# Causal mask of a fused attention block: a minimum on VectorE in place of mask products on TensorE, with the tile sums and the ends of the stages reordered

## The chip, the cores and the metric

The kernel runs on one core of one Trainium2 chip. The metric is device time in microseconds (us) of one execution; lower is better. TensorE is called PE below (PEld is its weight loads), VectorE DVE, ScalarE ACT, GpSimd POOL, and SyncE, which issues the DMAs here, SP.

## What is computed

Two rows of 2048 tokens of width 256 go through a pre-norm attention layer of 16 heads of width 64, and then through a linear layer:

```python
qkv = layernorm(x) @ W_qkv                       # [2, 2048, 3 * 1024]
score = einsum('bihd,bjhd->bijh', q, k) / 8
mask = tril(ones((l, l)))                        # keys after the query are left out
wmat = softmax(score * mask + 1e30 * (mask - 1), axis=2)
x = x + einsum('bijh,bjhd->bihd', wmat, v).reshape(b, l, 1024) @ W_out
W2 = W + up_aux @ (lora_up @ (lora_down @ down_aux))
x = x + layernorm(x) @ W2.T + b
```

## The kernel before

The kernel is written with an explicit order for each engine and explicit semaphores; nothing is scheduled by a tool. It has three stages, each one a block in which all engines run their own lists; between two blocks all engines wait for each other.

**First stage** (`project_qkv`): layernorm, then q, k and v for 8 tiles of 512 tokens. ACT and DVE copy each product out of PSUM into three stage buffers each, SP stores them (line 249). At the end of SP's list, lines 258 to 260 wait until every store has landed. Near the end the stage already loads q and k of the first item and finds its row maxima.

**Second stage** (`attention`): 16 items, one for each pair of heads and batch row. An item has 40 units (t, j): for each tile t of 512 queries (t from 0 to 3) the blocks j of 128 keys, j from 0 to 4t + 3. Units are numbered s, tile t starting at s = 0, 4, 12, 24. The last four units of a tile lie on the diagonal; they are called d0 to d3 here, and need 512, 384, 256 and 128 query columns for each of the two heads. For a unit

- PE makes the scores (`score_unit`, L791: four terms for each head, the last adds minus the row maximum), and on the diagonal adds four small products (L798, the constants `late_keys` and `pick`) that put -3e38 where the key comes after the query;
- ACT takes the exponential into one of 8 buffers `probs` (L921);
- PE multiplies by v into `o_acc` (`pv_unit`, L855);
- the sum of the exponentials is built: by POOL for the units before the diagonal (L1093, into `sum_pool`), by DVE on the diagonal (L1012 in tile 0, L1018 for d0, which reads `sum_pool`, and L1023 for d1 to d3, into `sum_dve`).

PE works in pairs of units: scores of the units s + 2 and s + 3, then the v products of s and s + 1. In between stand the row-maximum products of the next item (`chunk`, L819 and, on their diagonal, L827) into a ring of three PSUM banks, placed by the fixed table of `plan_chunks` (written "B" for a whole chunk and "s" for a narrow one); DVE reduces each (L990), and frees its bank thereby. In the last item nothing follows, so there are none.

Once a tile is summed, PE adds over the partitions (`denominators`, L865), ACT copies the row (L950), SP spreads it over the partitions through DRAM, DVE takes the reciprocal (L1043), SP brings it back (L713), POOL normalises (`normalise`, L1077, ten units into the next tile), and SP stores the tile of o (L699). POOL also makes the low halves of q and k for the next item at eight fixed units (L676, units 3, 8 to 11 and 20 to 22). The last item also splits W_out and loads and splits the first tile of o for the third stage (L722, L943, L1037).

POOL starts the sum of a tile (unit j = 1) once DVE has read `sum_pool` in d0 of the tile before.

**Third stage** (`project_and_ffn`): for 8 tiles of 512 tokens the output projection (`out_project`, L1271), layernorm and the linear layer (L1294). ACT and DVE split each tile of o into a high and a low half first (L1335, L1371). The last tile of o of the stage before is finished at its start (`finish_last_o`, L1223 to L1236), and only behind it SP loads the tiles 2 and 3 of o (L1191).

DVE's list for a unit, before:

```python
for here in places[1:] if s % 2 else places[:1]:
    for k in here:
        reduce_chunk(...)
if j >= NB * t:
    add_unit(n, s)
for late in late_tile(n, s - 5, previous):
    reciprocals(*late)
```

## Time and profile before

| | us |
|---|---|
| median of 3 runs (1955.82 to 1957.56) | 1955.83 |
| the profiled execution, its own time | 1958.16 |
| its span, first to last instruction | 1955.9 |
| PE busy | 1839.4 (94%) |
| DVE busy | 1247.7 (64%) |
| POOL busy | 1073.3 (55%) |
| ACT busy | 806.6 (41%) |

The first stage takes the time up to about 313 us, the second from there to about 1790, the third the rest. "Busy" of PE is modelled and counts overlapping instructions once. The mean granted PE clock is 0.987 of full speed.

### The profile page before, as it was taken

Reading aid. Unit: us, or ns where it says so; the run is one execution under the profiler, and the core shown is the slowest. Engines: PE = TensorE matmul, PEld = TensorE weight load, DVE = VectorE, ACT = ScalarE, POOL = GpSimd, SP = SyncE. Lnnn points to the kernel's source line nnn. Section 1 sums busy time; section 2 is a strip of 40 time slices with the busy share of each in tenths; the row PEclk is TensorE's granted clock in tenths of the full one; section 3 lists DMA queues with packets and bytes.
Section 4 is the critical chain, followed back from the end, with each engine's and each line's share of the span. In section 5 each row is a group of like instructions: output and inputs, shape, how many; then the busy total and the mean of one; then the engine's idle time right before and its main releaser. Section 6 shows DMA issues by size and latency. Waiting matters only on the chain. (4 is left out here: it accounts for less than half of the span.)

```text
span 1955.9 us, 34245 instructions
## 1 busy us (share of the span) xinstructions
PE 1839.4 (94%) x13464; PEld 1130.9 (58%) x13464; DVE 1247.7 (64%) x2024; ACT 806.6 (41%) x982; POOL 1073.3 (55%) x583
## 2 busy tenths in 40 slices
PE   7999998999999999999999999999999999997798
PEld 5877775555555555555555555555555555545697
DVE  5465643767676767667676767676767677632465
ACT  3222123444545454544545454545454545453121
POOL 1001002767586857667676767686867667575111
PEclk9999998999999999999999999999999999998899
DMA  5646445212121221212121212121221211031451
GB/s 204 227 175 227 162 167 173 66 45 66 50 66 56 59 66 45 66 45 78 54 73 37 77 39 72 45 69 47 66 72 45 66 45 50 18 117 47 172 194 54
DMA packets 150782, 171.33 MB, mean 88 GB/s; under 512 B 44618, under 2 KB 91744, under 8 KB 150624
## 3 DMA queue, kind: packets, MB, share of 16 engines
q1 hardware_dynamic: 150624, 169.15, 27.4%
q8 instruction: 108, 1.77, 0.4%
q14 instruction: 50, 0.41, 0.1%
HBM read 97.02 MB, written 71.57 MB: 86 GB/s over the span
## 5 line engine op out<-in xcount | busy, mean ns | idle before, releaser
L990 DVE TENSOR_REDUCE f_part_max<-b_ring 128x1 f32<-128x512 f32 (+3 forms) x1200 | 675.2, 604 | 323.6 <-PE b_ring L819 224.3
L921 ACT ACTIVATE b_probs<-b_scores 128x1024 f32<-128x1024 f32 (+3 forms) x640 | 567.5, 899 | 611.9 <-PE b_scores L791 357.6
L1093 POOL TENSOR_TENSOR b_sum_pool<-b_sum_pool,b_probs 128x1024 f32<-128x1024 f32 x288 | 687.0, 2385 | 61.6 <-ACT b_probs L921 31.3
L791 PE MATMUL b_scores<-f_split 64*128 64x512 f32 (+2 forms) x1920 | 269.6, 383 | 9.1 <-ACT b_probs L921 5.5
L791 PE MATMUL b_scores<-b_split 64*128 64x512 f32 (+2 forms) x1920 | 269.2, 382 | 2.8 <-ACT b_probs L921 2.6
L855 PE MATMUL b_o_acc<-b_probs,f_v_in 128*64 128x512 f32 (+3 forms) x1280 | 270.5, 544 | 0.0
L855 PE MATMUL b_o_acc<-b_probs,b_v_in 128*64 128x512 f32 (+3 forms) x1280 | 269.0, 541 | 0.0
L1093 POOL TENSOR_TENSOR b_sum_pool<-b_probs 128x1024 f32<-128x1024 f32 x48 | 116.0, 2417 | 264.0 <-ACT b_probs L921 264.0
L1023 DVE TENSOR_TENSOR g_sum_dve<-g_sum_dve,b_probs 128x768 f32<-128x768 f32 (+2 forms) x192 | 231.3, 1205 | 30.2 <-ACT b_probs L921 24.4
L791 PEld LDWEIGHTS b_scores<-b_split 64*128 64x128 f32 x1920 | 166.3, 186 | 50.5 <-issue 21.2
L791 PEld LDWEIGHTS b_scores<-f_split 64*128 64x128 f32 x1920 | 168.0, 187 | 45.8 <-issue 21.1
L819 PE MATMUL b_ring<-b_split 64*128 64x512 f32 (+2 forms) x640 | 142.8, 433 | 28.3 <-DVE f_part_max L990 27.6
L348 DVE COPY a_stage_d<-a_made 128x512 f32<-128x512 f32 x96 | 66.2, 691 | 142.1 <-PE a_made L293 142.0
L819 PEld LDWEIGHTS b_ring<-b_split 64*128 64x128 f32 x640 | 64.8, 183 | 146.7 <-issue 143.3
L819 PE MATMUL b_ring<-f_split 64*128 64x512 f32 (+2 forms) x560 | 125.5, 434 | 25.6 <-DVE f_part_max L990 24.8
L348 ACT COPY a_stage_a<-a_made 128x512 f32<-128x512 f32 x96 | 56.5, 589 | 225.6 <-PE a_made L293 225.6
L855 PEld LDWEIGHTS b_o_acc<-b_probs,b_v_in 128*64 128x64 f32 x1280 | 77.8, 136 | 111.2 <-issue 86.7
L855 PEld LDWEIGHTS b_o_acc<-b_probs,f_v_in 128*64 128x64 f32 x1280 | 77.9, 136 | 110.1 <-issue 86.8
L819 PEld LDWEIGHTS b_ring<-f_split 64*128 64x128 f32 x560 | 57.0, 184 | 128.8 <-issue 126.1
L791 PE MATMUL b_scores<-f_shift,p_first_row 64*128 64x512 f32 (+2 forms) x640 | 120.3, 364 | 0.0
L791 PE MATMUL b_scores<-b_shift,p_first_row 64*128 64x512 f32 (+2 forms) x640 | 120.2, 363 | 0.0
L676 POOL TENSOR_TENSOR b_split<-f_raw,b_split 128x512 fp32r<-128x512 f32 x64 | 81.5, 1297 | 54.8 <-ACT b_split L903 54.8
(135 smaller groups left out, 2250.4 us busy)
## 6 DMA issues: line engine op xcount, KB each, us to landing
f_raw<-k_t SPq DMA_DIRECT2D x32, 512.0 KB, 4.8
f_raw<-q_t SPq DMA_DIRECT2D x32, 512.0 KB, 5.6
g_recip<-r_t SPq DMA_DIRECT2D x128, 128.0 KB, 3.0
o_t<-g_o_norm SPq DMA_DIRECT2D x64, 256.0 KB, 2.0
q_t<-a_stage_a SPq DMA_DIRECT2D x32, 256.0 KB, 2.3
q_t<-a_stage_d SPq DMA_DIRECT2D x32, 256.0 KB, 2.1
k_t<-a_stage_a SPq DMA_DIRECT2D x32, 256.0 KB, 2.0
k_t<-a_stage_d SPq DMA_DIRECT2D x32, 256.0 KB, 2.0
```

The source lines that it names most:

```text
L348: copy(stage[e][s][:], made[:, g % BANKS, :]).then_inc(emptied[e], 1)
L676: vec.tensor_tensor(lo[u][:, cols], raw[p][:, which, inner], halves(hi[u][:, cols]), ALU.subtract).then_inc(split_lo, 1)
L791: last = nc.tensor.matmul(scores[s % 2][:, h, lo:TILE], lhs, b[u][head(h), queries], start=(term == 0), stop=(term == 3 and not diagonal))
L819: last = nc.tensor.matmul(rowwise[h][:, 0:wide], q_hi[u][head(h), ib * P:(ib + 1) * P], k_hi[u][head(h), c * TILE:c * TILE + wide], start= ...
L855: last = nc.tensor.matmul(o_acc[head(h), off:], v_in[u][:, j, head(h)], probs[s % PR][:, h, off:], start=(j == 0), stop=(j == NB * t + NB ...
L921: nc.scalar.activation(probs[s % PR][:, :, off:], scores[s % 2][:, :, off:], ACT.Exp, scale=scale).then_inc(exp_done, 1)
L990: nc.vector.tensor_reduce(part_max[:, h, ib, c:c + 1], rowwise[h][:, 0:width], AX.X, ALU.max).then_inc(chunk_reduced, 1)
L1023: nc.vector.tensor_tensor(sum_dve[t % 2][:, :, off:], sum_dve[t % 2][:, :, off:], probs[s % PR][:, :, off:], ALU.add).then_inc(dve_added, 1)
L1093: nc.gpsimd.tensor_tensor(sum_pool[:], first, probs[s % PR][:], ALU.add).then_inc(pool_added, 1)
```

## The change

The mask products L798 of the scores go. Instead DVE takes, for each diagonal unit, the minimum of the square of 128 by 128 exponentials (both heads) and a constant `allowed`, which is 3e38 where the key is allowed and 0 where it isn't. PE's v product of a diagonal unit and DVE's own add wait for that (`cleared`). DVE does the minimum as the first thing of its unit, ahead of the chunk reductions.

```diff
-                    diagonal = j >= NB * t
...
-                    if diagonal:
-                        for side in range(2):
-                            cols = slice(off + side * D, off + (side + 1) * D)
-                            for h in range(2):
-
-                                last = nc.tensor.matmul(scores[s % 2][:, h, cols], late_keys(h, side),
-                                                        consts["pick"][head(h), :], start=False, stop=(side == 1))
...
-                    pe.wait_ge(exp_done, n * U + s + 1 + 2)
+                    if j >= NB * t:
+                        pe.wait_ge(cleared, clear_before[n, s] + 1)
+                    else:
+                        pe.wait_ge(exp_done, n * U + s + 1 + 2)
...
+                def clear_later_keys(n, s):
...
+                    dve.wait_ge(exp_done, n * U + s + 1 + 2)
+                    nc.vector.tensor_tensor(probs[s % PR][:, :, off:off + P], probs[s % PR][:, :, off:off + P], allowed[:],
+                                            ALU.min).then_inc(cleared, 1)
...
+                        if j >= NB * t:
+                            clear_later_keys(n, s)
```

POOL's first add of a tile waits until DVE has finished the whole sum of the tile before, not only its d0:

```diff
-                                pool.wait_ge(dve_added, n * DIAG + NB * (t - 1) + 1 + NB)
+                                pool.wait_ge(dve_added, sum_ready[n, t - 1])
```

In the last tile of the last item DVE adds also the last four units ahead of the diagonal (j = 8 to 11), starting its own sum there, and adds POOL's sum once, behind d1. In the last item POOL normalises four units earlier:

```diff
+    LATE_FULL = 4
+    def dve_adds(n, s):
+        t, j = units[s]
+        return j >= NB * t or (n == LAST_ITEM and t == TI - 1 and j >= NB * t - LATE_FULL)
...
-                        for late in late_tile(n, s - 10, previous):
+                        for late in late_tile(n, s - (10 if following else 6), previous):
                             normalise(*late)
```

The waits for the first stage's stores move from the end of its SP list to the start of the second stage's, ahead of the loads of q and k of the second item. In the third stage SP issues the loads of o for the tiles 2 and 3 ahead of `finish_last_o`, and the load of x for tile 2 behind it:

```diff
                 load_x(0, 0)
+
+                wait_apart(sp, o_lo_ready, PARTS, first_loaded[0], 16)
...
-                finish_last_o()
-
-                wait_apart(sp, o_lo_ready, PARTS, first_loaded[0], 16)
                 load_o(2, 0, slice(0, KC), o_loaded[0])
-                step(0, 0, True, True, False)
+                step(0, 0, True, False, False)
+                finish_last_o()
+                wait_apart(sp, x1_ready, 1 + 2, first_loaded[0], 16)
+                load_x(2, 0)
```

How the lists stand. DVE in tile 1 of an item, from d0 on, before (L990 reduces chunks, L1018 and L1023 are the adds of d0 to d3, L1043 the reciprocal):

```order
L1018 TENSOR_TENSOR g_sum_dve<-b_sum_pool,b_probs 128x1024
L990 TENSOR_REDUCE f_part_max<-b_ring 128x1 x2
L1023 TENSOR_TENSOR g_sum_dve<-g_sum_dve,b_probs 128x2x384
L1043 RECIPROCAL g_recip_spread<-g_den_spread 128x8
L990 TENSOR_REDUCE f_part_max<-b_ring 128x1 x2
L1023 TENSOR_TENSOR g_sum_dve<-g_sum_dve,b_probs 128x2x256
L990 TENSOR_REDUCE f_part_max<-b_ring 128x1 x2
L1023 TENSOR_TENSOR g_sum_dve<-g_sum_dve,b_probs 128x2x128
```

The same place in the changed kernel (L1037 is the minimum, L1017 reduces, L1055 and L1060 are the adds, L1086 the reciprocal):

```order
L1037 TENSOR_TENSOR b_probs<-b_probs,b_allowed 128x2x128
L1017 TENSOR_REDUCE f_part_max<-b_ring 128x1 x2
L1055 TENSOR_TENSOR g_sum_dve<-b_sum_pool,b_probs 128x1024
L1037 TENSOR_TENSOR b_probs<-b_probs,b_allowed 128x2x128
L1017 TENSOR_REDUCE f_part_max<-b_ring 128x1 x2
L1060 TENSOR_TENSOR g_sum_dve<-g_sum_dve,b_probs 128x2x384
L1086 RECIPROCAL g_recip_spread<-g_den_spread 128x8
L1037 TENSOR_TENSOR b_probs<-b_probs,b_allowed 128x2x128
L1017 TENSOR_REDUCE f_part_max<-b_ring 128x1 x2
L1060 TENSOR_TENSOR g_sum_dve<-g_sum_dve,b_probs 128x2x256
L1037 TENSOR_TENSOR b_probs<-b_probs,b_allowed 128x2x128
```

Four minimums stand in the list now; that of d1 stands right behind the add of d0.

POOL's list of the last item, tiles 1 to 3, before (L1093 adds, L1077 normalises the tile before):

```order
L1093 TENSOR_TENSOR b_sum_pool<-b_sum_pool,b_probs 128x1024 x2
L1077 TENSOR_TENSOR g_o_norm<-g_o_raw,g_recip 128x512
L1093 TENSOR_TENSOR b_sum_pool<-b_probs 128x1024
L1093 TENSOR_TENSOR b_sum_pool<-b_sum_pool,b_probs 128x1024
L1077 TENSOR_TENSOR g_o_norm<-g_o_raw,g_recip 128x512
L1093 TENSOR_TENSOR b_sum_pool<-b_sum_pool,b_probs 128x1024 x5
L1077 TENSOR_TENSOR g_o_norm<-g_o_raw,g_recip 128x512
L1093 TENSOR_TENSOR b_sum_pool<-b_probs 128x1024
L1093 TENSOR_TENSOR b_sum_pool<-b_sum_pool,b_probs 128x1024 x9
L1077 TENSOR_TENSOR g_o_norm<-g_o_raw,g_recip 128x512
L1093 TENSOR_TENSOR b_sum_pool<-b_sum_pool,b_probs 128x1024
```

The same in the changed kernel (L1138 adds, L1123 normalises):

```order
L1138 TENSOR_TENSOR b_sum_pool<-b_sum_pool,b_probs 128x1024
L1123 TENSOR_TENSOR g_o_norm<-g_o_raw,g_recip 128x512
L1138 TENSOR_TENSOR b_sum_pool<-b_sum_pool,b_probs 128x1024
L1123 TENSOR_TENSOR g_o_norm<-g_o_raw,g_recip 128x512
L1138 TENSOR_TENSOR b_sum_pool<-b_probs 128x1024
L1138 TENSOR_TENSOR b_sum_pool<-b_sum_pool,b_probs 128x1024 x5
L1123 TENSOR_TENSOR g_o_norm<-g_o_raw,g_recip 128x512
L1138 TENSOR_TENSOR b_sum_pool<-b_sum_pool,b_probs 128x1024
L1138 TENSOR_TENSOR b_sum_pool<-b_probs 128x1024
L1138 TENSOR_TENSOR b_sum_pool<-b_sum_pool,b_probs 128x1024 x5
L1123 TENSOR_TENSOR g_o_norm<-g_o_raw,g_recip 128x512
L1138 TENSOR_TENSOR b_sum_pool<-b_sum_pool,b_probs 128x1024
```

The last tile has 7 adds in place of 11, and each normalisation now stands ahead of adds that it stood behind.

## Rows read from the trace of the kernel before

**Rows 1.** The page, part 1: busy us (share of the span) xinstructions.
```profile
PE 1839.4 (94%) x13464; PEld 1130.9 (58%) x13464; DVE 1247.7 (64%) x2024; ACT 806.6 (41%) x982; POOL 1073.3 (55%) x583
```
**Rows 2.** Line 1012, one copy for each item: duration, first and last start.
```profile
L1012 DVE COPY g_sum_dve<-b_probs x16: 694/694/695, 319.3 to 1704.6; 128x1024 f32<-128x1024 f32 x16
```
**Rows 3.** Waits of the whole span: us in total, times, longest us.
```profile
PE b_ring L819 <- DVE f_part_max L990: 52.4, 71, 1.0
```
**Rows 4.** Timeline of PE, item 5, tile 1: start us, us, instruction [idle before].
```profile
804.47 0.23 PE L798 MATMUL b_scores<-p_pick,p_late_keys 64*128 64x64 bf16 x4
804.54 0.60 PE L791 MATMUL b_scores<-b_split 64*128 64x256 f32 x6
...
805.54 1.73 PE L855 MATMUL b_o_acc<-b_probs,b_v_in 128*64 128x512 f32 x8
...
814.05 0.50 PE L819 MATMUL b_ring<-f_split 64*128 64x512 f32 x2 [0.81 <-DVE f_part_max L990]
```
**Rows 5.** Timeline of DVE, the same stretch.
```profile
811.36 2.34 DVE L1023 TENSOR_TENSOR g_sum_dve<-g_sum_dve,b_probs 128x256 f32<-128x256 f32 x1
```
**Rows 6.** Timeline of POOL, the same stretch.
```profile
803.36 1.28 POOL L1077 TENSOR_TENSOR g_o_norm<-g_o_raw,g_recip 128x512 f32<-128x512 f32 x1
804.60 1.28 POOL L676 TENSOR_TENSOR f_split<-f_raw,f_split 128x512 fp32r<-128x512 f32 x1
811.02 2.39 POOL L1093 TENSOR_TENSOR b_sum_pool<-b_probs 128x1024 f32<-128x1024 f32 x1 [5.14 <-ACT b_probs L921]
```
**Rows 7.** Line 1023: duration ns min/median/max over its three widths.
```profile
L1023 DVE TENSOR_TENSOR g_sum_dve<-g_sum_dve,b_probs x192: 424/943/2569, 323.9 to 1790.0; 128x768 f32<-128x768 f32 x64, 128x512 f32<-128x512 f32 x64, 128x256 f32<-128x256 f32 x64
```
**Rows 8.** Groups by line and shape: busy us, mean ns of one, idle before.
```profile
L1023 DVE TENSOR_TENSOR g_sum_dve<-g_sum_dve,b_probs 128x256 f32<-128x256 f32 x64 | 116.3, 1817 | 2.0
```
**Rows 9.** Timeline of the last item, tile 2: PE, DVE, POOL.
```profile
1748.85 1.72 PE L855 MATMUL b_o_acc<-b_probs,b_v_in 128*64 128x512 f32 x8
...
1749.89 1.23 DVE L1018 TENSOR_TENSOR g_sum_dve<-b_sum_pool,b_probs 128x1024 f32<-128x1024 f32 x1 [5.62 <-POOL b_sum_pool L1093]
1751.22 3.19 DVE L1023 TENSOR_TENSOR g_sum_dve<-g_sum_dve,b_probs 128x768 f32<-128x768 f32 x3
...
1750.63 1.63 POOL L1077 TENSOR_TENSOR g_o_norm<-g_o_raw,g_recip 128x512 f32<-128x512 f32 x1 [0.85 <-DMA g_recip<-r_t]
```
**Rows 10.** The last item, tile 1: timeline of PE, then windows (PEclk third from last).
```profile
1733.18 1.08 PE L865 MATMUL b_ring<-g_sum_dve,p_ones 128*64 128x512 f32 x4 [2.42 <-DVE g_sum_dve L1023]
...
1734.00:1736.00 2.00, 2.00 (x12) 1.49 (x12) 0.00 (x0) 0.62 (x2) 0.00 (x0) 0.65 0.45 126
1736.00:1738.00 2.00, 2.00 (x10) 1.01 (x10) 0.00 (x0) 1.32 (x2) 1.90 (x2) 0.50 0.00 0
```
**Rows 11.** Timeline of the end of the second stage: PE's last products, DVE, the third stage.
```profile
1779.43 2.37 PE L855 MATMUL b_o_acc<-b_probs,b_v_in 128*64 128x512 f32 x16
...
1786.81 1.22 DVE L1018 TENSOR_TENSOR g_sum_dve<-b_sum_pool,b_probs 128x1024 f32<-128x1024 f32 x1 [13.67 <-POOL b_sum_pool L1093]
...
1790.89 0.55 PE L1271 MATMUL c_y<-f_shift,f_split 128*128 128x256 f32 x1 [9.08 <-DVEq L1407]
```
**Rows 12.** Window of the third stage: length, busy of PE, PEld, DVE, ACT, POOL; PEclk; DMA.
```profile
1791.00:1796.00 5.00, 5.00 (x24) 5.00 (x25) 1.52 (x1) 3.44 (x1) 0.00 (x0) 0.50 0.72 210
```
**Rows 13.** Timeline of the third stage: SP, ACT, DVE and PE.
```profile
1823.25 0.37 SPq L1191 DMA_DIRECT2D f_raw<-o_t  x1
...
1817.39 1.02 ACT L1345 COPY c_xt<-c_turned 128x1024 f32<-128x1024 f32 x1 [3.96 <-PE c_turned L1282]
1832.38 3.60 ACT L1335 CAST f_split<-f_raw 128x4096 fp32r<-128x4096 f32 x1 [13.97 <-DMA f_raw<-o_t]
...
1836.02 4.42 DVE L1371 TENSOR_TENSOR f_split<-f_raw,f_split 128x4096 fp32r<-128x4096 f32 x1 [20.04 <-ACT f_split L1335]
...
1840.49 0.80 PE L1271 MATMUL c_y<-f_shift,f_split 128*128 128x256 f32 x2 [14.23 <-DVE f_split L1371]
```
**Rows 14.** Timeline of ACT at the start of the second stage.
```profile
322.07 1.04 ACT L903 CAST b_split<-f_raw 128x1024 fp32r<-128x1024 f32 x1 [2.84 <-DMA f_raw<-q_t]
```

102 lines of the change are left out of this document (69 added, 33 removed).

## The prediction

> **What bounds the kernel now.** I read the page first, then PE's waits over the whole span, then the timeline of one item around its tile ends, then the two block borders. The page shows PE busy for 1839.4 us, 94% of the span, with the next engine, DVE, at 64% [rows 1]: whatever takes work or idle time from PE counts in full, and nothing else does. The second stage is regular: the copy that opens each item starts at 319.3 in the first and 1704.6 in the last, so an item takes (1704.6 - 319.3)/15 = 92.35 us [rows 2]. One wait of PE inside the items matters: for a bank of the ring that DVE has yet to reduce, 52.4 us in 71 places, none over 1.0 us [rows 3]; over 15 items with a ring that is 3.5 us each.
>
> Where that comes from is seen at the end of tile 1 of item 5. POOL starts the next tile's sum at 811.02 and needs 2.39 us [rows 6]. DVE's add of d3 starts at 811.36, right behind it, and takes 2.34 us [rows 5], though the shortest add of line 1023 takes 0.424 us [rows 7]. POOL's add ends at 813.41; 813.41 - 811.36 = 2.05, and about 0.3 more is DVE's own work. So DVE stood until POOL was done, and the chunk reduction behind it kept PE waiting 0.81 us [rows 4]. It is the rule, not an exception: the 64 adds of this shape have a mean of 1817 ns [rows 8]. In these rows an add of DVE and an operation of POOL never run side by side; the one that is there first holds the other up for its whole length.
>
> **The mask products.** They go from PE. Four of them stand between 804.47 and 804.54 [rows 4]: 0.07 us a unit, since they run behind the larger ones. 16 units an item give 1.1 us, 16 items 18 us, all on PE's path.
>
> **POOL held behind DVE's sum.** The add of d3 then finds no POOL add, and takes about 0.45 us for 1.82 [rows 7, 8]. The ring waits should go nearly all: -3.5 us an item [rows 3]. POOL's first add starts about 1 us later, and so do the splits and the normalisation behind it; POOL's slack (1073.3 us busy of 1955.9 [rows 1]) covers that inside the tile, but these later operations now lie where the diagonal is.
>
> **The minimum.** The trace has no minimum. It has the shape of the smallest add of line 1023 (128x256, two operands in SBUF), so it is bounded by 0.42 us below (that add undisturbed) and 2.57 us above (the longest add of that line, which stood behind POOL) [rows 7]; I take 0.42 of its own, and work out its waits one by one. DVE has room for 16 x 0.42 = 6.7 us an item. For PE what counts is when the minimum is done, since the v product of a diagonal unit waits for it now. That of d0 and of d2 have a pair's scores as cover. That of d1 stands right behind the add of d0 on DVE, and the v product of d1 is due 0.9 us after that of d0. So the add of d0 (1.23 us undisturbed [rows 9]) enters PE's path, and with it whatever holds the add.
>
> Replay of tile 1 of item 5, all by durations of the rows. POOL's chain there ended with a split, a normalisation at 803.36 and a split at 804.60, 1.28 us each [rows 6]; by the later first add it stands some 0.6 us later, while PE, without picks and ring waits, comes 1.4 us earlier, the products of 805.54 [rows 4] at 804.15. The add of d0 is ready at 804.1, and finds the normalisation on (to 805.2): it ends at 806.3. POOL's last split, waiting since 805.2, then goes first, ahead of the minimum of d1: 807.55, minimum 807.85. PE wants it at 805.06: a wait of 2.9 us with the semaphore. In tile 2 the same replay gives 2.15, and 0.2 for d3. In tiles 0 and 3 the exponential and POOL's last add are both over by some 2 to 3 us when the products are due: nothing. Sum +5.25 us an item. If DVE kept the port from the add of d0 to the minimum, each wait would be about 0.65 us: these are the ends of this term, +1.3 and +5.25, and from the upper end on a lost clock (below). I take 5.25, since in the last item's tile 2 POOL's normalisation, waiting since 1750.63, did go between DVE's adds: three adds took 3.19 us, where the widest takes 0.94 undisturbed and the narrowest 0.42 [rows 7, 9], so about 1.1 of it was POOL's.
>
> By the Trainium skill, "SBUF — State Buffer", section "Who interferes with whom", the port pair is an exclusive lock that goes to whoever issues first, for the whole instruction. By that rule, the trace agrees for the adds. Taken to the letter, POOL's split, waiting since 805.2, goes ahead of the minimum, which gives the 5.25; were the lock given to DVE each time, the sum would be the fast rival's below.
>
> An item: -1.1 - 3.5 + 5.25 = +0.6; 15 items: **+9 us**.
>
> **The last item and the end of the stage.** Before, PE waited 2.42 us there for the sum of a tile, and the granted clock then showed 0.65 and 0.50 of full speed for 4 us [rows 10], which is 2 x 0.35 + 2 x 0.5 = 1.7 us lost: my price of such a fall. POOL's earlier normalisation takes this wait away, and the minimums bring two waits of 1.8 and 1.0 in the same tile by the same replay: -2.4 - 1.7 + 2.8 = -1.3. In tile 2 the add of d0 waited 5.62 us for POOL's sum, to 1749.89, and nothing of PE hung on it; the v product of d1 came at about 1748.85 + 0.9 = 1749.8 [rows 9]. Now the normalisation stands ahead of POOL's last add and the minimum of d1 behind the add of d0: 1749.89 + 1.3 + 1.23 + 0.4 = 1752.8, 3 us late. PE arrives some 2 us earlier too (1.3 as above, and 0.7 of picks by then), while POOL, which adds without a break there, does not: +5, and a fall, +1.7. Picks -1.1. Last item: +4.3; its ends are -1.1 - 4.1 = -5.2, if POOL is out of the way in both tiles, and +6.
>
> At its end PE is done with the products at 1781.8, but DVE starts on POOL's late sum at 1786.81, and PE starts the third stage at 1790.89, 9.08 us idle [rows 11]. In the changed kernel POOL has four adds of 2.4 us fewer, and DVE adds its sum once, behind d1, so what is left behind the last product is one small add and the border itself, about 1.95 us: -7.1. The slow clock of 0.50 in the 5 us after the gap [rows 12] is then not due: -2.6. Last item and border together: **-5.4**.
>
> **The third stage.** SP issues the load of the second tile of o at 1823.25, behind the finishing of the last tile; ACT waits 13.97 us for it (1832.38), DVE splits from 1836.02, and PE stands from 1826.3 to 1840.49, 14.23 us [rows 13]. Moved ahead, the load is issued at about 1794.3 and has landed long before ACT is free behind its copy of 1817.39: high half 1818.4 to 1822.0 (3.60), low half to 1826.5 (4.42), PE on at 1826.6. So -13.9, and the slow start behind the gap goes (as at the block border: -1.6), +0.3 for ACT and DVE being in the way of a smaller step: **-15.2**. Moved back on SP's list are the finishing of the last tile and the load of x of tile 2, both needed only many us later. The load shares the DMA engines with the weights issued at the start; it took 9.1 us before, from 1823.25 to ACT's start, and has 24 us now.
>
> **Between the first and second stage.** The stores' waits now stand ahead of the second item's loads. ACT still waits 2.84 us for the first loads of this stage until 322.07 [rows 14], and those loads wait on the same stores. I take **-0.3**; the ends are 0 and -2.84. The constant `allowed` is made by POOL at the start, covered by the same wait.
>
> **The sum.** The profiled execution took 1958.16, 2.3 above the median 1955.83. 1958.16 - 0.3 + 9 - 5.4 - 15.2 = 1946.3, which is 11.9 less; against the median, 1955.83 - 11.9 = **1944**.
>
> **The rivals.**
> *Slower: the clock falls at the new wait.* The wait of 2.9 us in tile 1 is longer than the one of 2.42 that was followed by a slow clock [rows 10]. If each costs a fall, 1.7 x 15 = 25 us more: 1969. If in tile 2 POOL's normalisation goes first too (+1.3) and the clock falls there (+1.7), 4.7 x 15 = 70 more: 2014. It decides from 0.8 us an item beyond my sum, since 11.9/15 = 0.79. For it: the idle time is longer and recurs. Against: the sum of d0 sits in a stretch where PE was fully busy before, and the last item, without the ring's products, may be special. Chance 0.27.
> *Faster: DVE keeps the port.* The waits are 1.3 us an item: 3.95 less, -59 at most; PE then runs earlier against ACT and some of it returns. With a quarter returned, about 45 less than my sum: 1899; halfway, where only one of the two tiles loses the race, 1922. For it: POOL needs a cycle through its own semaphore between operations, DVE doesn't. Against: the 3.19 us of [rows 9]. Chance 0.25.
> *No change: the ends give nothing.* The third stage's gap could stay, if the early load waits for its buffer or for the weights on the DMA engines; then 15.2 is missing: 1959, or 1955 where a fourth of it comes. For it: only that the load is a big one. Against: the 24 us. Chance 0.08.
> The forecast, 1937 to 1951, has 0.40.
>
> **How the numbers follow.** The range takes the fast rival in at its lower end, 1899, rounded to 1900, and the first half of the slow one, 1969, to 1975; what is left out is the doubled clock fall and a fast case without any return. A measurement of this kernel can tell about 0.2%, 3.9 us. Faster by over that (below 1951.9): 0.40 - 0.05 for a forecast missed towards the border, + 0.25 = 0.60; the slow rival ends above 1959.7 nearly always, and with the slow end of the no-change case: 0.27 + 0.04 = 0.31; same: 0.04 + 0.05 = 0.09.
>
> **What would show it.** Right: L798 gone; the add of 128x256 near 0.45 us; L819's wait for DVE nearly gone; new waits of PE's v products for the minimum (L1037), 2 to 3 us each in tiles 1 and 2, none in 0 and 3; items of about 93 us between the copies; PE's gap near 1826 gone, and the one at the border down to about 2 us. Each of these at another size mis-sizes its own term. Slow rival: granted clock below full speed behind the waits. Fast rival: minimums of d1 that start right behind the add of d0, items near 89.5. Wrong altogether: items unchanged with the waits gone, which would mean that another engine than PE paces them.

## The result, and the profile after

The changed kernel takes 1999.98 us (median of 4 runs, 1997.09 to 2007.53), the kernel before 1956.69 in the same measurement: a ratio of 1.0226, 95% interval 1.0196 to 1.0256. It is slower by 2.3%. The forecast was 1944, range 1900 to 1975. The profiled execution took 1997.09 us with a span of 1995.1, 39.2 more than the 1955.9 before.

Part 1 of the page, to be held against [rows 1]:

```profile
PE 1856.7 (93%) x12440; PEld 1116.3 (56%) x12440; DVE 1355.8 (68%) x2285; ACT 802.7 (40%) x982; POOL 1102.1 (55%) x582
```

PE has 1024 instructions fewer (256 units of 4 mask products) and is "busy" 17 us longer. That can't be more work: work went away, and the granted clock was lower (0.97 for 1.00 of full speed between 340 and 1680 us). The waits of PE over the whole span, beside [rows 3] (engine, tile, line, releaser: us in total, times, longest):

```profile
PE b_o_acc L886 <- DVE b_probs L1037: 83.4, 40, 6.3
PE b_scores L826 <- ACT b_probs L948: 15.0, 16, 6.1
...
PE b_ring L847 <- DVE f_part_max L1017: 8.6, 26, 1.7
```

The ring waits went from 52.4 us to 8.6 as forecast, and 83.4 us of waiting for the minimum came. Item 5, tile 1 again, beside [rows 4 to 6]; PE, then DVE, then POOL:

```profile
816.92 1.08 PE L886 MATMUL b_o_acc<-b_probs,b_v_in 128*64 128x512 f32 x4
...
820.69 1.34 PE L886 MATMUL b_o_acc<-b_probs,b_v_in 128*64 128x384 f32 x4 [2.69 <-DVE b_probs L1037]
```
```profile
816.91 2.33 DVE L1055 TENSOR_TENSOR g_sum_dve<-b_sum_pool,b_probs 128x1024 f32<-128x1024 f32 x1
819.16 1.48 DVE L1037 TENSOR_TENSOR b_probs<-b_probs,b_allowed 128x256 f32<-128x256 f32 x1
```
```profile
816.89 1.26 POOL L1123 TENSOR_TENSOR g_o_norm<-g_o_raw,g_recip 128x512 f32<-128x512 f32 x1
818.12 2.24 POOL L709 TENSOR_TENSOR f_split<-f_raw,f_split 128x512 fp32r<-128x512 f32 x1
...
827.53 2.38 POOL L1138 TENSOR_TENSOR b_sum_pool<-b_probs 128x1024 f32<-128x1024 f32 x1 [7.18 <-DVE g_sum_dve L1060]
```

This is the replay of the prediction, instruction by instruction. The add of d0 and POOL's normalisation start together (816.91 and 816.89); POOL works 1.26 us and the add is done after 2.33. POOL's split then goes ahead of the minimum of d1, which takes 1.48 us for 0.42 of its own. PE waits 2.69 us, where the prediction had 2.9. The last row shows the hold: POOL's first add starts at 827.53, behind DVE's whole sum, and the 128x256 add, 1817 ns in the mean before [rows 8], is cheap:

```profile
L1060 DVE TENSOR_TENSOR g_sum_dve<-g_sum_dve,b_probs 128x256 f32<-128x256 f32 x64 | 26.7, 417 | 0.6
```

What came on top is in the clock. Windows of 2 us around this wait, and around the end of that of tile 2 (852.5); the third number from the right is the granted clock:

```profile
819.00:821.00 2.00, 0.31 (x2) 0.20 (x4) 2.00 (x4) 0.00 (x0) 1.35 (x1) 0.99 0.40 133
821.00:823.00 2.00, 2.00 (x12) 0.84 (x10) 1.75 (x5) 0.00 (x0) 0.00 (x0) 0.50 0.00 0
823.00:825.00 2.00, 2.00 (x14) 1.58 (x14) 1.77 (x4) 0.39 (x1) 0.00 (x0) 0.66 0.07 2
852.00:854.00 2.00, 1.51 (x6) 0.32 (x6) 2.00 (x5) 0.00 (x0) 0.16 (x1) 0.50 0.52 160
...
856.00:858.00 2.00, 2.00 (x12) 1.57 (x10) 0.42 (x2) 1.02 (x1) 0.00 (x0) 0.50 0.63 205
```

The clock falls from 2.4 to 1.2 GHz at the wait and stays there for 3.4 us. In the 15 items with a ring there are 30 waits for the minimum of d1, of 1.57 to 2.69 us; at 21 of them such a slow stretch begins, between 0.9 us before the wait's end and 1.7 us behind it, and a 22nd came behind a ring wait of 1.69 us; five of the 22 are twice as long as the others, 6.8 us for 3.4.

Slow time multiplied by what is missing of full speed gives 46.1 us in the items, 27 times 1.7. The clock cost less than that, as is seen between items of one run that have like waits: 1.2 us in experiment 6, 1.5 in experiment 3, and 1.35 here for a further 3.4 us (items 6 and 12, with 6.8 us of slow clock, took 96.2 and 96.3; items 3, 5, 8 and 11, with 10.2, took 97.6). By these prices the clock cost 32 to 41 us.

To compare kernels I cut every trace at the same places: the first v product of item 0, that of item 15, PE's last v product, PE's first product of the third stage. The first two start at 325.2 and 1706.4 before (92.09 an item, where the prediction had 92.35 by DVE's copies); after:

```profile
323.59 1.97 PE L886 MATMUL b_o_acc<-b_probs,f_v_in 128*64 128x512 f32 x3
...
1756.51 1.72 PE L886 MATMUL b_o_acc<-b_probs,b_v_in 128*64 128x512 f32 x8
```

| us | before | after | difference |
|---|---|---|---|
| to item 0 | 325.2 | 323.6 | -1.6 |
| one item (15 of them) | 92.09 | 95.53 | +3.44, in all +51.6 |
| of it, by the clock | 0 | 2.2 to 2.7 | +32 to 41 in all |
| last item | 75.4 | 86.8 | +11.4 |
| border gap of PE | 9.1 | 1.1 | -8.0 |
| third stage | 165.1 | 150.7 | -14.4 |
| span | 1955.9 | 1995.1 | +39.2 |

The two block borders and the third stage gave 24 us; the items took 51.6, of which 32 to 41 is the clock, and the last item 11.4.

### The profile page after: what moved, and what is told of

It is laid out like the page before. It is cut to its first block and busy times, and to the rows that moved or that the text cites. A ratio compares the mean times of both kernels' runs of the same rounds, so it can differ in the third digit from the quotient of the medians.

```text
span 1995.1 us, 32457 instructions
## 1 busy us (share of the span) xinstructions
PE 1856.7 (93%) x12440; PEld 1116.3 (56%) x12440; DVE 1355.8 (68%) x2285; ACT 802.7 (40%) x982; POOL 1102.1 (55%) x582
## 5 line engine op out<-in xcount | busy, mean ns | idle before, releaser
L1017 DVE TENSOR_REDUCE f_part_max<-b_ring 128x1 f32<-128x512 f32 (+3 forms) x1200 | 675.9, 605 | 340.7 <-PE b_ring L847 245.6
L1138 POOL TENSOR_TENSOR b_sum_pool<-b_sum_pool,b_probs 128x1024 f32<-128x1024 f32 x284 | 678.0, 2387 | 37.0 <-POOL b_sum_pool L1138 1.4
L886 PE MATMUL b_o_acc<-b_probs,b_v_in 128*64 128x512 f32 (+3 forms) x1280 | 281.5, 555 | 45.0 <-DVE b_probs L1037 44.8
L886 PE MATMUL b_o_acc<-b_probs,f_v_in 128*64 128x512 f32 (+3 forms) x1280 | 279.2, 552 | 38.7 <-DVE b_probs L1037 38.6
L1138 POOL TENSOR_TENSOR b_sum_pool<-b_probs 128x1024 f32<-128x1024 f32 x48 | 115.1, 2398 | 324.7 <-DVE g_sum_dve L1060 303.2
L826 PE MATMUL b_scores<-f_split 64*128 64x512 f32 (+2 forms) x1920 | 274.0, 391 | 12.6 <-ACT b_probs L948 10.8
L826 PE MATMUL b_scores<-b_split 64*128 64x512 f32 (+2 forms) x1920 | 273.2, 390 | 4.3 <-ACT b_probs L948 4.2
L1037 DVE TENSOR_TENSOR b_probs<-b_probs,b_allowed 128x256 f32<-128x256 f32 x256 | 194.2, 759 | 27.2 <-ACT b_probs L948 26.2
L826 PEld LDWEIGHTS b_scores<-f_split 64*128 64x128 f32 x1920 | 173.6, 194 | 54.8 <-ACT b_probs L948 19.4
L826 PEld LDWEIGHTS b_scores<-b_split 64*128 64x128 f32 x1920 | 172.0, 192 | 57.6 <-issue 20.3
L1060 DVE TENSOR_TENSOR g_sum_dve<-g_sum_dve,b_probs 128x768 f32<-128x768 f32 (+3 forms) x196 | 145.6, 743 | 3.2
```

Of the source, the lines that this page charges most:

```text
L826: last = nc.tensor.matmul(scores[s % 2][:, h, lo:TILE], lhs, b[u][head(h), queries], start=(term == 0), stop=(term == 3))
L886: last = nc.tensor.matmul(o_acc[head(h), off:], v_in[u][:, j, head(h)], probs[s % PR][:, h, off:], start=(j == 0), stop=(j == NB * t + NB ...
L1017: nc.vector.tensor_reduce(part_max[:, h, ib, c:c + 1], rowwise[h][:, 0:width], AX.X, ALU.max).then_inc(chunk_reduced, 1)
L1037: nc.vector.tensor_tensor(probs[s % PR][:, :, off:off + P], probs[s % PR][:, :, off:off + P], allowed[:], ALU.min).then_inc(cleared, 1)
L1060: nc.vector.tensor_tensor(sum_dve[t % 2][:, :, off:], sum_dve[t % 2][:, :, off:], probs[s % PR][:, :, off:], ALU.add).then_inc(dve_added, 1)
L1138: nc.gpsimd.tensor_tensor(sum_pool[:], first, probs[s % PR][:], ALU.add).then_inc(pool_added, 1)
```

## The experiments

All ratios are against runs of the kernel before on the same chip; the cuts are those of the table above. "Clock" is the slow time in the 15 items multiplied by what was missing of full speed, in us: 1.7 for a stretch of 3.4 us, more than it cost.

| kernel | median | ratio (95%) | item | waits for min / ring, tiles 1 and 2, an item | clock |
|---|---|---|---|---|---|
| changed | 1999.98 | 1.0226 (1.0196-1.0256) | 95.53 | 4.67 / 0.4 | 46.1 |
| minimums of a pair first | 1944.7 | 0.9948 (0.9932-0.9965) | 92.28 | 0 / 4.6 | 1.7 |
| POOL not held | 1967.57 | 1.0068 (1.0050-1.0086) | 93.40 | 2.50 / 0 | 0 |
| before, POOL held | 1927.65 | 0.9863 (0.9847-0.9880) | 89.92 | - / 1.46 | 8.5 |
| before, block ends | 1942.51 | 0.9933 (0.9917-0.9950) | 92.11 | - / 0.7 | 0 |
| reductions, then adds | 1960.61 | 1.0022 (1.0012-1.0032) | 93.29 | 0 / 4.9 | 10.2 |
| first in tile 1 alone | 1963.55 | 1.0043 (1.0029-1.0058) | 93.12 | 2.06 / 2.4 | 15.4 |
| POOL behind the minimum | 2088.32 | 1.0673 (1.0655-1.0691) | 101.66 | 2.7 / 7.2 | 81.9 |
| normalisation back | 1994.68 | 1.0221 (1.0181-1.0260) | 95.39 | 4.63 / 0.3 | 46.1 |
| minimum between | 1959.65 | 1.0019 (0.9995-1.0043) | 93.70 | 0.7 / 3.4 | 32.4 |
| products kept | 1905.9 | 0.9749 (0.9733-0.9766) | 89.95 | - / 1.36 | 10.2 |
| products kept, early norm. | 1911.91 | 0.9761 (0.9733-0.9788) | 90.19 | - / 1.50 | 11.9 |
| POOL light | 1885.38 | 0.9636 (0.9620-0.9652) | 88.23 | 1.02 / 0 | 0 |
| products kept, POOL light | 1870.0 | 0.9554 (0.9538-0.9570) | 87.67 | - / 0 | 0 |

(The ring waits at tile starts, 2.8 us an item, are there where POOL isn't held.)

**1. The minimum ahead of the add.**

```diff
-                        if j >= NB * t:
+                        if j >= NB * t and s % 2 == 0:
                             clear_later_keys(n, s)
+                            clear_later_keys(n, s + 1)
```

> The changed kernel with one thing moved: on DVE both minimums of a pair of diagonal units come first, so that of d1 stands ahead of the add of d0 and not behind it. Theory A (PE waits for the minimum of d1 because it stands behind an add that has to wait for POOL, and each such wait is followed by a slow clock): PE's wait for the minimums falls from 83.4 us to under 10, the slow-clock stretches inside the items go, an item takes about 92.1 - 1.1 (picks) - 2.8 (ring waits) = 88.2 us for 95.5, and the time is about 1998 - 15 x 7.3 - 8 in the last item = 1880 us. Theory B (256 minimums and a later POOL load the shared port, wherever they stand): the total of DVE's and POOL's work is the same, so items stay above 94 and the time above 1970.

Measured: 1944.7. The wait for the minimum is gone in the items, and so is the slow clock (1.7 us of it left), which is theory A. But the item takes 92.28 and not 88.2, so neither theory's number was hit: PE waits for the ring instead.

```profile
PE b_ring L847 <- DVE f_part_max L1017: 71.2, 93, 1.5
...
PE b_o_acc L886 <- DVE b_probs L1037: 10.3, 4, 5.3
```

Its DVE shows why: the two minimums take 2.88 us together, and the reductions stand behind them.

```profile
801.08 2.88 DVE L1037 TENSOR_TENSOR b_probs<-b_probs,b_allowed 128x256 f32<-128x256 f32 x2
803.88 1.27 DVE L1017 TENSOR_REDUCE f_part_max<-b_ring 128x1 f32<-128x512 f32 x2
805.08 2.31 DVE L1055 TENSOR_TENSOR g_sum_dve<-b_sum_pool,b_probs 128x1024 f32<-128x1024 f32 x1
```

So A holds for the clock and for where the wait was, and B has a share: as long as something holds DVE there, order only chooses who waits.

**2. Without the hold.**

```diff
-                                pool.wait_ge(dve_added, sum_ready[n, t - 1])
+                                pool.wait_ge(dve_added, sum_pool_read[n, t - 1] if t > 1 else dve_before[n, 0] + 1)
```

> The changed kernel, but POOL's first add of a tile waits only for DVE's read of its sum, as in the kernel before. Theory A: POOL's splits and normalisation stand about 1 us earlier, but still beside the add of d0, and PE meets the ring waits again; the waits for the minimum fall to 1.5 to 2.5 us each in tiles 1 and 2, and are still followed by a slow clock: items of 94 to 96 us, 1985 to 2005 in all. Theory C (holding POOL is what pushed its work into the diagonal, and alone makes the loss): the waits for the minimum fall below 0.7 us, no slow clock, items of about 92, 1945.

Measured: 1967.57, between the two theories, with the waits and the clock as neither had them. The waits for the minimum of d1 are 1.11 and 1.39 us in the mean, and none of them was followed by a slow stretch. Windows of this run, from just before the wait in item 5's tile 1 and tile 2 on:

```profile
812.00:816.00 4.00, 2.98 (x26) 1.98 (x28) 4.00 (x9) 0.61 (x1) 0.69 (x1) 1.00 0.08 4
842.00:846.00 4.00, 3.28 (x28) 2.04 (x28) 3.86 (x10) 0.98 (x2) 0.00 (x0) 1.00 0.94 199
```

The hold makes each wait about 1.1 us longer (2.35 and 2.32), and with the longer waits the slow clock comes. That the lengthening is due to PE coming sooner and POOL's splits later was argued and not tested apart.

**3. The hold alone**, in the kernel before.

```diff
-                                pool.wait_ge(dve_added, n * DIAG + NB * (t - 1) + 1 + NB)
+                                pool.wait_ge(dve_added, n * DIAG + NB * t + NB)
```

> The kernel before, with POOL held behind the whole of DVE's sum and nothing else. Theory A: PE's ring waits fall from 52.4 us to under 12 (8.6 in the changed kernel), nothing of PE waits for the sum of a diagonal, items take 92.1 - 2.8 = 89.3 us and the time is about 1956 - 42 = 1914 us. Theory C: the later POOL work costs PE elsewhere (exponentials wait for their buffer, sums come late): items stay above 91.5 and the time above 1945.

Measured: 1927.65, 1.4% faster. The items go from 92.09 to 89.92. The ring waits at the tile starts are gone; one of 1.46 us in the mean stays at d2 of tile 1; after five of them, each of 1.94 to 1.96 us, the clock is slow (after the longest, 2.43, it is not). Items 4, 6, 8 and 12 with such a fall took 91.4 to 91.5, item 10 with the same wait and none took 89.9: a fall cost 1.5 us. The 1914 expected was missed by 14 us: the item came out 0.6 longer (9 us in all, the falls among it), and the border gap of PE grew from 9.08 to 11.97. The last cell of a 2 by 2 is now full (item, us): before 92.09, hold 89.92, minimum 93.40, both 95.53. Added up, hold and minimum would give 91.23; together they cost 4.3 us more, of which some 2 are the clock.

**4. The block ends alone**, in the kernel before: the waits for the stores moved, the loads of o ahead of `finish_last_o`.

```diff
                 load_x(0, 0)
+                wait_apart(sp, o_lo_ready, PARTS, first_loaded[0], 16)
...
-                finish_last_o()
-                wait_apart(sp, o_lo_ready, PARTS, first_loaded[0], 16)
                 load_o(2, 0, slice(0, KC), o_loaded[0])
-                step(0, 0, True, True, False)
+                step(0, 0, True, False, False)
+                finish_last_o()
+                wait_apart(sp, x1_ready, 1 + 2, first_loaded[0], 16)
+                load_x(2, 0)
```

> The kernel before, with only the waits for the stores moved and the third stage's loads reordered. Expected from the changed kernel's trace: first stage's border -1.8 us, third stage -14.3, nothing else: 1956 - 16 = 1940 us, PE's 14.2 us gap gone. Rival: the first border's gain came from the rest of the change (none of it here), then 1942; or the load of o takes its time from the border's other loads, then above 1945.

Measured: 1942.51, 0.7% faster; to item 0 it is 1.1 us less, the third stage 13.6. The gap of [rows 13] is gone from PE's waits, the border gap stays (8.8), since its part of the change isn't in this kernel.

**5. Adds behind both reductions.** DVE's order for a pair: two minimums, the reductions of both units, the two adds; in the last item four minimums before the adds, and the normalisation at its old place.

```diff
+                        if j >= NB * t and s % 2 == 0:
+                            clear_later_keys(n, s)
+                            clear_later_keys(n, s + 1)
                         for here in places[1:] if s % 2 else places[:1]:
...
                         if dve_adds(n, s):
-                            add_unit(n, s)
+                            waiting.append(s)
+                        if s % 2 and (following or j != NB * t + 1):
+                            for unit in waiting:
+                                add_unit(n, unit)
+                            waiting = []
```

> The changed kernel with DVE's order for each pair of diagonal units: both minimums, then the chunk reductions of both units, then both adds (in the last item all four minimums ahead of the four adds), and POOL's normalisation of the last item at its old place. Theory A (what costs is everything that PE waits for standing behind the add of d0, which meets POOL; with the minimums alone ahead, the ring's reductions paid it instead, 4.6 us an item in the run before): minimums and ring waits both under 0.7 us an item, no slow clock in the items; an item 92.1 - 1.1 - 2.8 = about 88.3 us, last item about 74 us for 86.8; in all 1998 - 15 x 7.2 - 12 = about 1878. Theory B (the shared port is loaded in any order): the reductions come in time but the adds run late and hold ACT's buffers or the denominators; items above 91, time above 1925.

Measured: 1960.61; theory A fails here by its number, and theory B's numbers hold (items above 91, time above 1925), but not its account, which had the reductions in time. The ring waits stay, 4.9 us an item. In tile 1 of item 5 the minimums themselves took 1.00 and 1.50 us for 0.42, each behind a split of POOL. Putting the adds last doesn't help when the first of DVE's two-operand instructions is already held.

**6. The minimum first in tile 1 alone.**

```diff
-                        if j >= NB * t:
+                        if j >= NB * t and t != 1:
                             clear_later_keys(n, s)
+                        if j >= NB * t and t == 1 and s % 2 == 0:
+                            clear_later_keys(n, s)
+                            clear_later_keys(n, s + 1)
```

> The changed kernel with the minimums of a pair ahead of the adds in tile 1 alone; tiles 2 and 3 as changed. Theory A (each wait of about 2 to 2.7 us is followed by its own slow stretch): PE's wait for the minimum of d1 in tile 1 goes (2.35 us an item), ring waits of some 2.4 us an item come in its place, in pieces; tile 2 keeps its 2.3 us. Slow stretches of 1.7 us fall from 27 to about 13 or 14: items 95.5 - 0.9 x 1.7 = about 94.0 us, 1975 in all. Rival (the clock falls because of both waits together): slow stretches under 4 in all, items about 92.5, 1952.

Measured: 1963.55, items of 93.12. Nine slow stretches, 15.4 us, between A's 13 and the rival's 4. Removing one of two waits an item removed more than half of them. The waits of the items 3 to 13 are nearly alike here: those with a fall took 93.45 to 93.77 us, those with none 92.41 to 92.49, so a fall cost 1.2 us in the mean.

**7. POOL's splits and normalisation behind the minimum of d1.**

```diff
+                        if t in (1, 2) and j == NB * t:
+                            pool.wait_ge(cleared, clear_before[n, s + 1] + 1)
                         if following and s in LO_SLOTS:
```

> The changed kernel, with POOL's splits and normalisation of tiles 1 and 2 held until the minimum of d1 is done, so that nothing of POOL can stand ahead of the add of d0 or of that minimum. Theory A (1.7 to 2.2 us of the wait are POOL's operation ahead of the add, and the one between add and minimum): the wait for the minimum falls from 2.35 and 2.32 us to about 0.6 each, and no slow clock follows; POOL's operations now meet the adds of d1 to d3 and cost ring waits of 1 us or so; items about 95.5 - 3.1 (clock) - 3.4 + 1 = 90 us, 1915 in all. Rival (the wait is DVE's own queue, the reductions and the add ahead of the minimum): the wait stays at 1.5 us or more in both tiles, items above 92.

The wait in question did what A says: 0.50 us in tile 1 and in tile 2, for 2.35 and 2.32. Yet the time is 2088.32. DVE of this run, tile 1:

```profile
850.59 1.22 DVE L1055 TENSOR_TENSOR g_sum_dve<-b_sum_pool,b_probs 128x1024 f32<-128x1024 f32 x1
851.72 0.42 DVE L1037 TENSOR_TENSOR b_probs<-b_probs,b_allowed 128x256 f32<-128x256 f32 x1
...
861.02 0.20 DVE L1086 RECIPROCAL g_recip_spread<-g_den_spread 128x8 f32<-128x8 f32 x1 [6.71 <-DMA g_den_spread<-g_den_row]
```
```profile
862.12 0.79 PE L847 MATMUL b_ring<-f_split 64*128 64x512 f32 x2 [6.68 <-DVE f_part_max L1017]
```

Add and minimum are free of POOL (1.22 and 0.42). But POOL's three splits start at 852.22, behind the minimum, and the normalisation only at 856.64. SP issues its store at 857.97 and behind it the small load of the denominators, for which the reciprocal on DVE waits 6.71 us, with the reductions behind it. I had costed this at ring waits of 1 us: the chain through SP was missed.

**8. The normalisation of the last item back at its place.**

```diff
-                        for late in late_tile(n, s - (10 if following else 6), previous):
+                        for late in late_tile(n, s - 10, previous):
```

> The changed kernel with POOL's normalisation of the last item at its old place, ten units into the next tile. As the prediction has it, the early normalisation of tile 1 stands ahead of POOL's last add of tile 2 there, and the minimum of d1 waits for it: the wait of 6.3 us falls by the 1.3 us of one normalisation to about 5, and the 2.4 us wait for the sum of tile 0 comes back: the last item stays within 2 us of 86.8. Rival (the early normalisation makes the 6.3 us wait): it falls below 3 us and the last item takes under 82 us.

The rival is right on the wait: that in tile 2 falls from 6.30 to 1.74 us. The last item falls only to 83.8, since the two waits in tile 1 grew from 3.1 to 3.9 us together and those of tile 3 from 2.9 to 3.7, so neither number of the last item was hit; the wait for the sum of tile 0 did not come back.

Where the 4.6 us come from is seen in the two traces. In both, one normalisation stands among POOL's adds of tile 2. In the changed kernel another one stands ahead of the first add, and waits for the load of its own reciprocals. The changed kernel, POOL, then DVE:

```profile
1783.88 1.27 POOL L1123 TENSOR_TENSOR g_o_norm<-g_o_raw,g_recip 128x512 f32<-128x512 f32 x1 [10.65 <-DMA g_recip<-r_t]
1785.11 2.40 POOL L1138 TENSOR_TENSOR b_sum_pool<-b_probs 128x1024 f32<-128x1024 f32 x1
...
1801.29 2.33 POOL L1138 TENSOR_TENSOR b_sum_pool<-b_sum_pool,b_probs 128x1024 f32<-128x1024 f32 x1
```
```profile
1779.97 0.42 DVE L1060 TENSOR_TENSOR g_sum_dve<-g_sum_dve,b_probs 128x256 f32<-128x256 f32 x1
...
1803.72 1.23 DVE L1055 TENSOR_TENSOR g_sum_dve<-b_sum_pool,b_probs 128x1024 f32<-128x1024 f32 x1 [5.82 <-POOL b_sum_pool L1138]
```

And POOL with the normalisation back:

```profile
1780.82 2.38 POOL L1138 TENSOR_TENSOR b_sum_pool<-b_probs 128x1024 f32<-128x1024 f32 x1 [9.38 <-DVE g_sum_dve L1060]
```

DVE's sum of tile 1 is done at 1780.4 in the changed kernel, and POOL's first add of tile 2 starts 4.7 us later: 3.5 of standing at the normalisation and 1.3 of doing it. With the normalisation back the add starts 0.1 us behind DVE's sum. POOL goes on almost without a break from there, and the wait of PE for the minimum of d1 is longer by as much, 6.30 us for 1.74.

**9. The minimum between.** On DVE: minimum of d0, its reductions, minimum of d1, add of d0; normalisation back.

```diff
-                        if j >= NB * t:
+                        if j >= NB * t and s % 2 == 0:
                             clear_later_keys(n, s)
...
+                        if j >= NB * t and s % 2 == 0:
+                            clear_later_keys(n, s + 1)
                         if dve_adds(n, s):
                             add_unit(n, s)
```

> The changed kernel with the minimum of d1 (and of d3) between the reductions of the even unit and the add of d0, so that it neither stands behind the add nor ahead of the reductions, and POOL's normalisation of the last item at its old place. Theory A: the wait for the minimum goes as with both minimums first (2.35 and 2.32 us an item to near nothing), and of the ring waits that came in its place there (4.6 us an item) the 1.4 and 0.7 us ahead of d0's product go too, since the reductions now come first; items 92.3 - 2.1 = about 90.2 us, 1912 in all. Theory B (the port is loaded in any order, the wait only moves): ring waits or waits for the minimum stay above 4 us an item and the items above 92, 1940 or more.

Measured: 1959.65, items of 93.70; B in its numbers (3.4 + 0.7 us of waits). The waits ahead of the product of d0 did go (1.41 to 0, 0.73 to 0.09), but those at d2 grew to 1.70 and 1.58 us, with 19 slow stretches. DVE, then POOL, of this run:

```profile
805.23 1.46 DVE L1037 TENSOR_TENSOR b_probs<-b_probs,b_allowed 128x256 f32<-128x256 f32 x1
806.61 1.27 DVE L1017 TENSOR_REDUCE f_part_max<-b_ring 128x1 f32<-128x512 f32 x2
807.81 1.52 DVE L1037 TENSOR_TENSOR b_probs<-b_probs,b_allowed 128x256 f32<-128x256 f32 x1
809.26 2.29 DVE L1055 TENSOR_TENSOR g_sum_dve<-b_sum_pool,b_probs 128x1024 f32<-128x1024 f32 x1
```
```profile
803.91 3.92 POOL L709 TENSOR_TENSOR f_split<-f_raw,f_split 128x512 fp32r<-128x512 f32 x3
807.79 1.27 POOL L1125 TENSOR_TENSOR g_o_norm<-g_o_raw,g_recip 128x512 f32<-128x512 f32 x1
809.01 1.45 POOL L709 TENSOR_TENSOR f_split<-f_raw,f_split 128x512 fp32r<-128x512 f32 x1
```

DVE's three instructions with two operands in SBUF each waited for one of POOL's: 1.46, 1.52 and 2.29 us where they need 0.42, 0.42 and 1.22, 3.2 us lost in all. Whichever stands last is late.

**10, 11. The mask products kept**, all else of the change; with the last item's normalisation at its old place, and at the new one.

```diff
+                    if diagonal:
+                        for side in range(2):
...
+                                last = nc.tensor.matmul(scores[s % 2][:, h, cols], late_keys(h, side),
...
-                    if j >= NB * t:
-                        pe.wait_ge(cleared, clear_before[n, s] + 1)
-                    else:
-                        pe.wait_ge(exp_done, n * U + s + 1 + 2)
+                    pe.wait_ge(exp_done, n * U + s + 1 + 2)
...
-                        if j >= NB * t:
-                            clear_later_keys(n, s)
```

> The changed kernel with the mask products on PE put back in place of the minimum; POOL still held, the last tile's adds shared with DVE, the block ends reordered; POOL's normalisation of the last item at its old place. From the runs so far: start of the items at 323.6, items of 89.9 us (as with POOL held alone), a last item of 73 to 74, a border gap of 1.1 and a third stage of 151: 323.6 + 1348.8 + 73.5 + 1.1 + 151 = 1898 for the span, a time of 1900 to 1903 us, the best so far. If the items get slower than 91, the rest of the change costs there too.

> The same, with the normalisation of the last item four units earlier as in the changed kernel. PE's product of d1 no longer hangs on DVE here, so the early normalisation can cost only through the sums: the wait of 1.0 us for the sum of tile 0 goes, nothing else comes; within 2 us of the run without it.

Measured: 1905.9 and 1911.91. The first is the best full kernel of this study, 2.5% faster than before, though 3 us over what I expected: the border gap is 6.4 us, not 1.1. PE is done with its products at 1746.5 there, and DVE's last adds end only at 1752.3:

```profile
1751.12 1.22 DVE L1062 TENSOR_TENSOR g_sum_dve<-g_sum_dve,b_probs 128x512 f32<-128x512 f32 x2
...
1752.81 0.77 PE L1313 MATMUL c_y<-f_shift,f_split 128*128 128x256 f32 x2 [6.35 <-DVEq L1449]
```

In the changed kernel DVE's last add ends at 1843.1, 0.3 us ahead of PE's last product, PE having waited 2.9 us for DVE's minimums in tile 3 by then. So the gap of 1.1 us is not the reordering's doing alone.

The medians of the two runs lie 6 us apart where I expected 2 at most. Their times overlap (1902.6 to 1914.04 against 1905.36 to 1910.01), so the time alone doesn't show that the early normalisation costs anything without the minimum. In the profile the last item was 3.2 us longer, and a wait of PE for the sum of tile 2 had grown from 0.4 to 3.1 us; POOL's first add of tile 2 stands behind a normalisation that waits for its load here too (10.30 us idle before it).

**12, 13. POOL's splits and normalisations made small**, in the changed kernel and in that of 10. Each works on 32 of its 512 columns; the rest of that work is left out, so these two kernels don't compute the layer, and their times serve as measurements only.

```diff
+            if vec is nc.gpsimd:
+                cols = slice(part * TILE, part * TILE + D // 2)
+                inner = slice(half * TILE, half * TILE + D // 2)
...
-                    nc.gpsimd.tensor_tensor(o_norm[:], o_raw[t % 2][:], recip[:], ALU.mult).then_inc(o_ready, 1)
+                    nc.gpsimd.tensor_tensor(o_norm[:, 0:D // 2], o_raw[t % 2][:, 0:D // 2], recip[:, 0:D // 2], ALU.mult).then_inc(o_ready, 1)
```

(The untouched columns are set to zero once, at the start of the stage.)

> The changed kernel, where each split of the next item's low halves and each normalisation on POOL works on 32 columns of its 512 (the rest of that work is left out, so the low halves and o are not those of the reference); every wait and the number of operations stay. Theory A (PE's waits come from POOL's full operations going on the shared port between DVE's): the wait for the minimum of d1 falls from 2.35 and 2.32 us to about 0.5 in each tile (DVE's add alone, as in the run with POOL's work held), the ring waits stay under 0.5, no slow clock in the items: items of 92.1 - 1.1 - 2.8 + 1.0 = about 89.2 us, 1998 - 15 x 6.3 = about 1903 in all. Theory B (DVE's own queue with 6.7 us more of work an item): waits for the minimum of 1 us or more stay, items above 91.

> The kernel with the mask products kept and POOL held, with the same work left out on POOL. Its waits of 1.4 us an item on the ring go, and the slow stretches: items 89.95 - 0.7 (clock) - 1.3 = about 88.0 us. Against the run with the minimum and the same work left out this shows the price of the minimum on a free port: by the prediction's terms 1.1 us of products saved against 1.0 to 1.3 of waits, so both within 1 us an item. If the minimum is dearer than that even here, then DVE's order and not POOL is what costs.

Measured: 1885.38 and 1870.0; items of 88.23 and 87.67, no slow stretch in either. The waits for the minimum of d1 are 0.51 us in both tiles, the ring waits in the diagonals are gone:

```profile
783.39 1.22 DVE L1058 TENSOR_TENSOR g_sum_dve<-b_sum_pool,b_probs 128x1024 f32<-128x1024 f32 x1
784.52 0.42 DVE L1040 TENSOR_TENSOR b_probs<-b_probs,b_allowed 128x256 f32<-128x256 f32 x1
```

The order, the waits and the number of instructions are those of the changed kernel, so 95.53 - 88.23 = 7.3 us an item is what POOL's operations beside DVE's cost it, clock included. With the products kept the same step gives 89.95 - 87.67 = 2.3. The other 5 us come from the minimum meeting POOL. With POOL's operations short, the minimum is still 0.56 us an item dearer than the products. This decides between A and B: DVE's list is as long as before, and the waits are gone. POOL's own list became shorter too, but what changed for DVE is how long its instructions last: the add of d0 takes 1.22 us for 2.33 and the minimum of d1 0.42 for 1.48, and in the rows of the changed kernel neither had DVE idle before it. Runs that shorten the operations and keep POOL's list as long were not made.

The last item doesn't follow: 83.3 us in experiment 12, with a wait of 4.37 us in tile 2, where POOL again stands at the early normalisation until its load has landed (1673.88, 11.03 us idle before it). That wait is not one for the port.

## Why the prediction was wrong

- **The mask products** (-1.1 us an item). From experiments 12 and 13: the minimum is 0.56 dearer, while it brings waits of 1.02 for the minimum, and 0.4 more at two other places; so the products give about 0.85. Slightly high.
- **The hold** (-3.5 of ring waits): -2.9, (52.4 - 8.6)/15. Near, but not all of it is the hold's doing: alone in the kernel before it took 2.0 us of ring waits an item (3.5 to 1.46) and 2.2 off the item.
- **The minimum** (+5.25 of waits): +4.67 (2.35 and 2.32; forecast 2.9 and 2.15). Right, mechanism, place and size; "POOL's last split, waiting since 805.2, then goes first" is the trace's own story.
- **The item** (+0.6): 3.44, less 2.2 to 2.7 of clock, is +0.7 to +1.3. The two items of the changed kernel that had no slow stretch, items 9 and 10, took 93.0 and 92.8 for 92.09 before; their waits were 1.57 to 1.95 us.
- **The clock** is the step that failed. The sum put it at nothing; the prediction had it as a rival with a chance of 0.27, at "1969" for one fall an item and "2014" for two. There were 1.8 times 3.4 us of slow clock an item, which cost 32 to 41 us in the 15 items. Its price of a fall, 1.7 us, was too high; 1.2 to 1.5 were measured. The argument against, that the wait "sits in a stretch where PE was fully busy before", was no evidence: nothing in the rows said that this protects the clock, and the one row there was [rows 10] showed a fall after 2.42 us of idling. With a replay that gave 2.9 us, the fall belonged in the sum.
- **The range** ended at 1975, in the middle of that rival. Its upper part, one mechanism with 0.27, should have been inside.
- **The last item** (+4.3): +11.4, the second step that failed. The wait of tile 2 was 6.3 us, where I had 3 us late and 2 of PE's earlier coming: the early normalisation was taken as 1.3 us of work, and it stood 3.5 us at its own load besides (experiment 8). With it came the slow clock (slow time multiplied by what is missing is 4.3 us in the last item, for 1.7 before) and three short waits in tile 3 (0.65, 0.52, 1.72), which I had not listed: there the add of POOL's sum stands between d1's and d2's minimum.
- **The border** (-7.1): -8.0, but this is partly luck. That "what is left behind the last product is one small add and the border itself" held with PE kept back by the minimums (2.9 us in tile 3); with the products kept the gap is 6.4 us (experiment 10). The slow clock behind it (-2.6) did not go: the window 1842 to 1847 shows 0.50, and the waits in tile 3 came right ahead of it.
- **The third stage** (-15.2): -14.4, and alone in the kernel before -13.6. Right, though the -14.4 holds what went of the slow clock at its start too. **The first border** (-0.3): -1.6, within its ends.
- **The fast rival** (DVE keeps the port) is dead: in item 5's tiles POOL got in ahead of the minimum each time.

The span came out 51 us above its forecast (+39.2 for -11.9). 42.6 of these lie in the items, 32 to 41 of them by the clock, and 7.1 in the last item.

By the Trainium skill, "SBUF — State Buffer", section "Who interferes with whom", the order of issue decides who blocks, and the one who is first holds the pair for the whole instruction. The rows of experiment 9 agree: POOL's normalisation, issued at 807.79, goes ahead of the minimum issued at 807.81, which takes 1.52 us for 0.42.

## What to carry to other kernels

An instruction taken off the bounding engine and given to one with idle time is dear if the bounding engine must wait for it: its price is then what stands ahead of it in its queue and what holds its port at that moment, and both were to be read in the trace before. Where the rows show a slow clock after an idle gap of PE, put its price in the sum for each new gap of that length: here 1.2 to 1.5 us for a fall, on top of waits of about 2 us. An instruction that is moved earlier in a list may stand there for its own data, and holds up all behind it: look up when they land. Measure the parts of a change apart: here the change without the minimum was worth 2.5%, and the minimum took all of it and 2.3% more.

## What was not expected of the hardware

- DVE and POOL, both with a list of instructions whose two operands are in SBUF, get in each other's way again and again: in experiment 9 the order of issue was split, minimum, split, normalisation, minimum, split, add, and each of DVE's three took 1.0 to 1.1 us more, whatever its own length (0.42 or 1.22). The price is what is left of POOL's operation (1.27 us) at that moment.
- The 30 waits of 0.5 to 1.6 us for the minimum in experiment 2 left the clock at 1.00; of 30 waits of 1.57 to 2.69 us in the changed kernel 21 had a fall at their end, one of 1.92 us among them, and two of 2.69 us had none. Length alone doesn't settle it, and what else does stays open.
- A fall of the clock cost less than its slow time multiplied by what is missing: 1.2 us (experiment 6), 1.35 (the changed kernel) and 1.5 (experiment 3) for a stretch of 3.4 us at half speed, which would be 1.7. Why is open.
